# Expert blocks in pairs, 512-wide operations, and the gate/up bias added on DVE

## The reference

```python
gu = jnp.einsum('th,ehf->tef', x, gate_up_proj) + gate_up_proj_bias
gate, up = gu[..., ::2], gu[..., 1::2]
gate = jnp.minimum(gate, LIMIT); up = jnp.clip(up, -LIMIT, LIMIT)
glu = gate * jax.nn.sigmoid(gate * ALPHA)
act = (up + 1.0) * glu
down = jnp.einsum('tei,eih->teh', act, down_proj) + down_proj_bias
out = jnp.einsum('te,teh->th', w, down)
```

## Time and profile before

| | us |
|---|---|
| median of 3 runs (lowest, highest) | 518.12 (512.25, 523.25) |
| the profiled execution: time | 514.28 |
| its span, first to last instruction | 512.5 |
| busy in the span: PE, DVE, POOL, ACT | 389.9, 372.8, 303.0, 221.1 |

### The profile page before, as it was taken

How to read it: one execution, slowest core, us unless ns; L and a number is a source line. 1 busy time by engine, 2 the same in 40 slices (tenths; PEclk the granted TensorE clock), 3 DMA queues, 4 the chain that set the end, 5 groups by cost and what they waited for, 6 DMA issues and landing times.

```text
span 512.5 us, 7809 instructions
## 1 busy us (share of the span) xinstructions
PE 389.9 (76%) x2269; PEld 331.8 (65%) x2269; DVE 372.8 (73%) x861; ACT 221.1 (43%) x480; POOL 303.0 (59%) x260
## 2 busy tenths in 40 slices
PE   0769757224599999999999999981788597888840
PEld 0668657223388889888888988861354386777730
DVE  7897786699387778888788777754997346657640
ACT  3463551000144544445454444531455266778441
POOL 6996890066656677777666667533445242554562
PEclk9866888555599999999999999995689668778665
DMA  6465751000322222322322323306920000111112
GB/s 215 159 203 152 239 149 42 0 0 1 92 74 91 82 88 87 99 91 91 91 87 84 94 72 95 83 25 223 347 87 1 0 1 1 42 41 66 60 41 82
DMA packets 32248, 45.82 MB, mean 89 GB/s; under 512 B 5998, under 2 KB 24818, under 8 KB 32210
## 3 DMA queue, kind: packets, MB, share of 16 engines
q0 software_dynamic: 7968, 21.90, 13.7%
q1 hardware_dynamic: 20018, 19.24, 12.0%
q10 hardware_dynamic: 4224, 4.19, 2.5%
HBM read 28.49 MB, written 17.69 MB: 90 GB/s over the span
## 4 chain that ended last, share of the span: by engine, by line
PE 58%; DVE 21%; ACT 6%; POOL 6%; issue 5%; DMA 3%; SPq 1%; DVEq 0%; POOLq 0%; ACTq 0%
PE bank L885 30%; DVE X L1359 6%; PE bank L882 5%; PE bank L876 3%; PE bank L901 3%; PE bank L846 3%; DVE gu_lo L1114 2%; DVE flow L1205 2%; DVE pair L1201 2%; POOL x_lo L512 2%; POOL pair L515 2%; DVE flow L1110 2%; PE bank L1016 2%; ACT quantT L786 1%; PE bank L825 1%
## 5 line engine op out<-in xcount | busy, mean ns | idle before, releaser
L564 POOL DMA_INDIRECT y_rows<-outs,slot_dst x71 | 71.6, 1009 | 51.2 <-issue 29.9
L544 POOL DMA_INDIRECT rows<-u_rows,slot_src x71 | 71.2, 1003 | 24.8 <-issue 19.2
L692 ACT ACTIVATE tanh<-gate 128x256 f32<-128x256 f32 x71 | 29.6, 417 | 99.8 <-DVE gate L1253 99.8
L885 PE MATMUL bank<-gu_hi,rowT_lo 128*128 x142 | 57.1, 402 | 0.0
L885 PE MATMUL bank<-gu_hi,rowT_hi 128*128 x142 | 56.7, 400 | 0.0
L885 PE MATMUL bank<-gu_lo,rowT_hi 128*128 x142 | 56.4, 397 | 0.0
L1253 DVE TENSOR_SCALAR gate<-bank 128x256 f32<-128x256 f32 x71 | 30.1, 424 | 24.4 <-PE bank L885 24.2
L677 ACT ACTIVATE rowT_hi<-bank 128x256 fp32r<-128x256 f32 x71 | 26.8, 378 | 40.0 <-PE bank L876 40.0
L1359 DVE SCALAR_TENSOR_TENSOR X<-picks,tok_w,X 128x256 f32<-128x256 f32 x64 | 38.9, 673 | 5.8 <-DMA picks<-y_rows 5.5
L1271 DVE TENSOR_TENSOR actT_lo<-bank,actT_hi 128x256 fp32r<-128x256 f32 x71 | 30.1, 424 | 15.3 <-ACT actT_hi L697 14.7
L885 PE MATMUL bank<-dn_lo,actT_hi 128*128 x142 | 40.2, 283 | 0.0
(11 more groups left out here) (268 smaller groups left out, 1196.8 us busy)
## 6 DMA issues: line engine op xcount, KB each, us to landing
picks<-y_rows SPq DMA_DIRECT2D x16, 512.0 KB, 7.2
X<-in_x SPq DMA_DIRECT2D x8, 512.0 KB, 5.7
raw_gu<-in_L_ffn_gate_up_proj SPq DMA_DIRECT2D x8, 512.0 KB, 4.2
u_rows<-flow ACTq DMA_DIRECT2D x8, 512.0 KB, 2.9
out<-X POOLq DMA_DIRECT2D x8, 512.0 KB, 3.4
raw_dn<-in_L_ffn_down_proj SPq DMA_DIRECT2D x8, 256.0 KB, 5.2
rows<-u_rows,slot_src POOLq DMA_INDIRECT x71, 2.8
y_rows<-outs,slot_dst POOLq DMA_INDIRECT x71, 2.5
```

The source lines that it names most:

```text
L544: pool.indirect_dma_start(out=rows[:, s, :], out_offset=None, in_=u_rows, in_offset=bass.IndirectOffsetOnAxis(ap=slot_src[:, n:n + 1], axi ...
L564: pool.indirect_dma_start(out=y_rows, out_offset=bass.IndirectOffsetOnAxis(ap=slot_dst[:, m:m + 1], axis=0), in_=outs[:, m % UNROLL, :], i ...
L692: a.activation(tanh[:, s % 2], gate[:, s % 2], ACT.Tanh, scale=ALPHA).then_inc(tanh_ready, 1)
L885: mm = pe.matmul(acc, left[:, part, :], right[:, ds(expert), part, :].rearrange("p e f -> p (e f)"), start=False, stop=(part == parts - 1 ...
```

## The change

Blocks are taken in pairs: 34 pairs and then 3 single blocks, 37 steps in all (`steps`). The rows' transposes of both blocks go into one bank (4), those of act into one bank (5), each 512 columns, so that ACT and DVE take both blocks in one operation. Gate/up products of the two blocks use two of the four banks 0 to 3, and the down products of the two share bank 6 or 7. The tiles gate, up, tanh, glu, act and actT have one buffer of 512 columns instead of two of 256. The gate/up product has no bias product any more: `gu_bias` now holds the bias in all partitions, put there by one broadcast DMA of SP (128 x 4096 x 4 bytes), and DVE adds it in `biased`, once per block 512 wide, out of PSUM into `gu_sum`, with the block's expert read into a register. The clips read `gu_sum`; the "+ 1" of up moves from the bias into the product with gate. The bias's first DMA, its clearing, splitting and four placing DMAs are gone.

In iteration g, PE does gate/up of the first block of g, the transposes of rows(g+1), down(g−2), gate/up of the second block of g, the transposes of act(g−1). ACT does the rounding of act(g−2), tanh(g−1), the rounding of rows(g+1), outs(g−2). DVE does the sum of the second block of g−1, the remainder of act(g−2), clips and product of g−1, the remainder of rows(g+1), act(g−1), the sum of the first block of g. POOL's loop keeps its order over blocks; its waits count steps. Lines taken away inside rewritten functions are left out below; they are in the listing above.

```diff
@@ -94,6 +94,12 @@
     UNROLL = 8
     NB = (2 * B * S - E) // P + E
     T = B * S
+    PAIR = 2
+    PAIRED = (NB - 2) // 2 * 2
+    steps = [[n, n + 1] for n in range(0, PAIRED, 2)] + [[n] for n in range(PAIRED, NB)]
+    STEPS = len(steps)
+    step_of = {n: g for g, blocks in enumerate(steps) for n in blocks}
+    step_first = lambda g: steps[g][0] if 0 <= g < STEPS else (NB if g >= STEPS else 0)
     GT = 8
     YR = 4
...
-        bank = [ctx.enter_context(nc.psum_tensor(f"bank{i}", [P, 512], F32)) for i in range(8)]
+        gu_banks = ctx.enter_context(nc.psum_tensor("gu_banks", [P, 4, 512], F32))
+        bank = [gu_banks[:, i] for i in range(4)] + [
+            ctx.enter_context(nc.psum_tensor(f"bank{i}", [P, 512], F32)) for i in range(4, 8)]
...
             dn_lo = sb("dn_lo", [P, E, KI, H], F32R)
-            gu_bias = sb("gu_bias", [P, 2, E, I], F32R)
+            gu_bias = sb("gu_bias", [P, E, GU])
             dn_bias = sb("dn_bias", [P, E, H], F32R)
             ones2 = sb("ones2", [P, P], F32R)
...
                 rows = sb("rows", [P, UNROLL, H])
-                rowT_hi = sb("rowT_hi", [P, 2, KH, P], F32R)
-                rowT_lo = sb("rowT_lo", [P, 2, KH, P], F32R)
-                gate = sb("gate", [P, 2, I])
-                up = sb("up", [P, 2, I])
-                tanh = sb("tanh", [P, 2, I])
-                glu = sb("glu", [P, 2, I])
-                act = sb("act", [P, 2, I])
-                actT_hi = sb("actT_hi", [P, 2, KI, P], F32R)
-                actT_lo = sb("actT_lo", [P, 2, KI, P], F32R)
+                rowT_hi = sb("rowT_hi", [P, 2, PAIR * H], F32R)
+                rowT_lo = sb("rowT_lo", [P, 2, PAIR * H], F32R)
+                gu_sum = sb("gu_sum", [P, 2, PAIR * I])
+                gate = sb("gate", [P, PAIR * I])
+                up = sb("up", [P, PAIR * I])
+                tanh = sb("tanh", [P, PAIR * I])
+                glu = sb("glu", [P, PAIR * I])
+                act = sb("act", [P, PAIR * I])
+                actT_hi = sb("actT_hi", [P, PAIR * I], F32R)
+                actT_lo = sb("actT_lo", [P, PAIR * I], F32R)
                 outs = sb("outs", [P, UNROLL, H])
...
-        W_DMAS, BIAS_DMAS, PLACE_DMAS = 2, 2, 6
+        W_DMAS, BIAS_DMAS, PLACE_DMAS = 2, 1, 2
...
@@ -439,16 +447,13 @@
             straight(B, 2, load)
-            sp.wait_ge(bias_step, 5)
-            sp.wait_ge(bias_cleared, 2)
+            sp.wait_ge(bias_step, 2)
+            sp.wait_ge(bias_cleared, 1)
             for half in range(2):
-                for two in range(2):
-                    part = E * GU // P // 2
-                    sp.dma_start(gu_bias[half:half + 1, two].bitcast(F32).rearrange("r e i -> r (e i)"),
-                                 flat_gb[:, half, two * part:(two + 1) * part].bitcast(F32)
-                                 ).then_inc(bias_placed, 16)
                 sp.dma_start(dn_bias[half:half + 1].bitcast(F32).rearrange("r e i -> r (e i)"),
                              flat_db[:, half, :].bitcast(F32)).then_inc(bias_placed, 16)
+            sp.dma_start(gu_bias[:].rearrange("p e f -> p (e f)"),
+                         gate_up_b.rearrange("e f -> (e f)").partition_broadcast(P)).then_inc(gu_bias_loaded, 16)
             sp.wait_ge(rowT_lo_ready, 1)
@@ -540,7 +545,8 @@
             for n in range(NB + AHEAD):
                 if n < NB:
                     s = n % UNROLL
-                    wait_count(pool, rowT_psum, n - UNROLL + 1)
+                    if n >= UNROLL:
+                        pool.wait_ge(rowT_psum, step_of[n - UNROLL] + 1)
                     pool.indirect_dma_start(
                         out=rows[:, s, :], out_offset=None, in_=u_rows,
...
                 if m >= 0:
-                    pool.wait_ge(outs_ready, m + 1)
+                    pool.wait_ge(outs_ready, step_of[m] + 1)
...
@@ -670,47 +676,40 @@
             a.wait_ge(slots_ready, 2)
...
+            def rows_rounded(g):
+                cols = len(steps[g]) * H
+                a.wait_ge(rowT_psum, g + 1)
+                a.activation(rowT_hi[:, g % 2, 0:cols], bank[4][:, 0:cols], ACT.Copy).then_inc(rowT_hi_ready, 1)
+            def activate(g):
+                cols = len(steps[g]) * I
+                a.wait_ge(gate_ready, g + 1)
+                a.activation(tanh[:, 0:cols], gate[:, 0:cols], ACT.Tanh, scale=ALPHA).then_inc(tanh_ready, 1)
+            def transposed_act(g):
+                cols = len(steps[g]) * I
+                a.wait_ge(actT_psum, g + 1)
+                a.activation(actT_hi[:, 0:cols], bank[5][:, 0:cols], ACT.Copy).then_inc(actT_hi_ready, 1)
+            def finish_down(g):
+                blocks = steps[g]
+                a.wait_ge(down_psum, g + 1)
+                for n in blocks:
+                    wait_count(a, outs_stored[n % UNROLL], 16 * (n // UNROLL))
+                first = blocks[0] % UNROLL
+                a.activation(outs[:, first:first + len(blocks), :].rearrange("p b h -> p (b h)"),
+                             bank[6 + g % 2][:, 0:len(blocks) * H], ACT.Copy).then_inc(outs_ready, 1)
+            rows_rounded(0)
+            for g in range(STEPS + 2):
+                if 0 <= g - 2 < STEPS:
+                    transposed_act(g - 2)
+                if 0 <= g - 1 < STEPS:
+                    activate(g - 1)
+                if g + 1 < STEPS:
+                    rows_rounded(g + 1)
+                if 0 <= g - 2 < STEPS:
+                    finish_down(g - 2)
             a.wait_ge(w1_loaded, 48)
...
@@ -869,70 +868,75 @@
                 mm.then_inc(turned, 1)
...
+            def rows_transposed(g):
+                for i, n in enumerate(steps[g]):
+                    pe.wait_ge(rows_loaded[n % UNROLL], 16 * (n // UNROLL + 1))
+                wait_count(pe, rowT_lo_ready, g)
+                for i, n in enumerate(steps[g]):
+                    for half in range(KH):
+                        mm = pe.transpose(bank[4][:, (i * KH + half) * P:(i * KH + half + 1) * P],
+                                          rows[:, n % UNROLL, half * P:(half + 1) * P], ident[:])
                 mm.then_inc(rowT_psum, 1)
...
+            def split_product(acc, hi, lo, w_hi, w_lo, expert, parts, begun):
                 for part in range(parts):
+                    cols = slice(part * P, (part + 1) * P)
                     for left, right in ((hi, w_hi), (lo, w_hi), (hi, w_lo)):
...
+                        mm = pe.matmul(acc, left[:, cols],
                                        right[:, ds(expert), part, :].rearrange("p e f -> p (e f)"),
...
+                                       start=(not begun and part == 0 and left is hi and right is w_hi),
+                                       stop=(part == parts - 1 and right is w_lo))
                 return mm
...
+            experts = {}
+            def gate_up(g, i):
+                d, own = g % 2, slice(i * H, (i + 1) * H)
+                n = steps[g][i]
+                if i == 0:
+                    wait_count(pe, sum_ready, step_first(g - 1))
+                    pe.wait_ge(rowT_lo_ready, g + 1)
+                    for m in steps[g]:
+                        experts[m] = pe.value_load(block_expert[0:1, m:m + 1], min_val=0, max_val=E - 1)
+                mm = split_product(gu_banks[:, 2 * d + i], rowT_hi[:, d, own], rowT_lo[:, d, own], gu_hi, gu_lo,
+                                   experts[n], KH, False)
+                mm.then_inc(gu_psum, 1)
+            def act_transposed(g):
+                pe.wait_ge(act_ready, g + 1)
+                wait_count(pe, actT_lo_ready, g)
+                for i in range(len(steps[g])):
+                    for half in range(KI):
+                        cols = slice((i * KI + half) * P, (i * KI + half + 1) * P)
+                        mm = pe.transpose(bank[5][:, cols], act[:, cols], ident[:])
                 mm.then_inc(actT_psum, 1)
...
+            def down(g):
+                pe.wait_ge(actT_lo_ready, g + 1)
+                wait_count(pe, outs_ready, g - 1)
+                for i, n in enumerate(steps[g]):
+                    own, expert = slice(i * I, (i + 1) * I), experts.pop(n)
+                    acc = bank[6 + g % 2][:, i * H:(i + 1) * H]
+                    pe.matmul(acc, ones2[:], dn_bias[:, ds(expert), :].rearrange("r e h -> r (e h)"), start=True, stop=False)
+                    mm = split_product(acc, actT_hi[:, own], actT_lo[:, own], dn_hi, dn_lo, expert, KI, True)
+                mm.then_inc(down_psum, 1)
             pe.wait_ge(experts_ready, 1)
             pe.wait_ge(slots_ready, 2)
             pe.wait_ge(bias_placed, 16 * PLACE_DMAS)
...
+            rows_transposed(0)
+            for g in range(STEPS + 2):
+                if g < STEPS:
+                    gate_up(g, 0)
+                if g + 1 < STEPS:
+                    rows_transposed(g + 1)
+                if 0 <= g - 2 < STEPS:
+                    down(g - 2)
+                if g < STEPS and len(steps[g]) == 2:
+                    gate_up(g, 1)
```

(62 more changed lines are left out.)

122 lines of the change are left out of this document (4 added, 118 removed).

## The result

The changed kernel takes **610.86 us** (median of 4 runs, 608.13 to 612.30); the kernel before took 520.64 beside it (4 runs, 512.25 to 523.25). The ratio is **1.185, interval 1.171 to 1.199**: slower, as forecast, but 32 us beyond the 579 and outside the range. The profiled execution of after took 612.3, its span 610.6.

A forecast was written before the change was run, and what follows sets the result against it. PE bounds the kernel at 2.89 us a block; after the change a ring through POOL's queue would. The stage adds 63.5 us, the start -0.5: 514.3 becomes 577, or 579 on a mean base; range 565 to 606.

The forecast's parts named there:

- chance of 0.68: Chance given to the forecast itself: the ring at 7.4 to 8.3 us a lap, 564 to 592 us.
- Ring, clean lap: POOL's queue: next pair's gather waits behind a scatter needing outs; 7.88 us a lap instead of 5.79, 30 laps.
- in a third or fewer of the laps: Rival of cold PE: clock drops behind the wait in only some laps, 580 to 600 us; chance 0.15.
- one 3.25 us hole: Evidence against cold PE: clock still 1.00 at 64 to 66 us, inside an idle stretch longer than the ring's 2.5 us.
- price per cold lap: Half clock doubles the ring's transposes and products, 0.43 + 1.52: +1.95 us a lap, +59 over 30; full case 638, chance 0.08.
- Fill: First pairs of the expert stage, before late rows set the laps; outs(0) was to end at 151.0 us.
- called register loads covered: Register loads, the sums and the moved wait for sums hide in each lap's idle time: PE 2.5 us, DVE 3.
- Start of the stage: Before the expert stage, bias memset and one SP issue go: 0.5 us earlier at best, taken as -0.5.
- End: From the end of outs(30) at 387.4 us through last pairs and singles to scatter 70: 22.9 us, so 410.3.
- DVE, ACT: Per pair DVE needs 4.9 us with sums at 0.68 each, ACT's four 512-wide copies 2.4; both hidden under the ring.
- The term for clips beside the gather: 512-wide clips on SBUF may lengthen the ring's gather: up to +0.25 us a lap, 7 in all, for the range only.
- PE-bound, faster: Rival: gather arrives in time before the rows' transposes, pairs take 5.32 us, 505 us on the mean base; chance 0.06.

The follow-up runs named there:

- e1: Changed kernel with scatter n-9 instead of n-8 issued behind gather n (AHEAD 9 instead of 8): 552.71 us, ratio 0.997 to the kernel before.
- e9: Changed kernel with gathers 7 blocks ahead instead of 8 (AHEAD 7): 727.63 us, ratio 1.305 to the kernel before.
- e4: Kernel before, single blocks, with gathers 4 blocks ahead instead of 8: 742.10 us, ratio 1.340 to the kernel before.
- e6: Changed kernel, unchanged, run again beside the kernel before on a later chip: 608.56 us, ratio 1.105.
- e3: Changed kernel plus eight unread 512-wide products on PE before its wait for rows of pairs 4 to 33: 595.53 us, ratio 1.077 to the kernel before.
- e11: Changed kernel plus four unread 512-wide products per pair on PE before its wait for rows: 595.72 us, ratio 1.066 to the kernel before.
- e12: Changed kernel, unchanged, run once more on a third later chip: 611.48 us, ratio 1.086 to the kernel before.
- e7: Changed kernel with scatter n-9 behind gather n and PE's expert register loads moved ahead of its waits: 551.25 us against 550.60 for the kernel before.
- e5: Kernel before, unchanged, profiled again on a later chip: 552.79 us.

## Why the prediction was wrong, and where it was right

Direction and mechanism held; the time did not, and the chance of 0.68 lay on the wrong case. The forecast for the profiled execution's span was 512.5 + 63.0 = 575.5; measured are 610.6, so +35.1 is to be found.

- **Ring, clean lap.** 7.88 forecast, 7.85 to 7.95 in 13 laps, every link within 0.1 (above). 30 waits of PE before the rows, as said. e1, e9 and e4 show the cause: one number in POOL's queue order makes and unmakes it.
- **The failed step: no term for the clock in the sum, "in a third or fewer of the laps" at a chance of 0.15.** The ring was forecast with every lap at full clock; 14 of 29 laps are cold. What their stretch from turned rows to ACT's outs takes beyond 2.33 us adds up to 15.1 of the +19.9 us on the 228.5 (e6 has 14 such laps and 15.0). My evidence against, one 3.25 us hole inside which the clock still was 1.00, was the wrong reading: it told of the clock in the hole, not of the clock that the work behind it got. What the row did show, 0.50 from 68 to 70 behind that hole, was the warning. The price per cold lap was too high: 1.95 forecast, 0.60 to 1.79 in after (mean 1.08), since in most of them the low clock covers only a part of the chain (mean granted clock 0.50 to 0.70 over the first 3.5 us); in e9 it is 1.2 to 1.8 (mean 1.64). Half the laps at about half the price made 15 us, where a third of them at the full price would make 19.5. So this is the largest term that was left out, but not the only one: 20 of the 35 us lie in the terms below. The Trainium skill, "TensorE: Matmul & The Clock Gate", section "HAM oscillation — how this bites in real kernels", tells of a kernel with DMA waits of some 3 to 5 us in which every burst behind one started cold. The trace agrees for the holes of 4.1 to 6.5 us in e9, in all laps. For the holes here, shorter than the page's, it happened in 14 of 29 laps.
- **The rest of the laps' +19.9**, 4.8 us: 2.4 for one late scatter, 1.0 for the late rows of the two laps named above (the same two laps have them in e3 and e11: 8.60 and 8.59, 8.33 and 8.55), and about 0.05 in each lap. The late scatter, in after's ACT and POOL timelines:

```profile
380.58 0.60 ACT L700 ACTIVATE outs<-bank 128x512 f32<-128x512 f32 x1 [2.36 <-PE bank L886]
```

```profile
384.38 1.14 POOL L570 DMA_INDIRECT y_rows<-outs,slot_dst  x1 [6.73 <-issue]
```

  From the end of outs to the scatter are 3.20 us, not 0.80. It is scatter 52, the 114th indirect DMA of POOL, and e3, e6, e11 and e12 have 3.20 or 3.21 at the same one. So has the kernel before (outs ends at 295.46, the scatter starts at 298.67): the delay is not the change's, but only the ring makes it cost time. Its cause is open.
- **Fill: +5.3.** From rows of pair 0 to rows of pair 4 I had 21.4 us; it took 26.7. In after's timeline the low part of the first rows ends at 141.72 + 0.69 = 142.41, and the first gate/up product starts 1.76 later:

```profile
141.72 0.69 DVE L1233 TENSOR_TENSOR rowT_lo<-bank,rowT_hi 128x512 fp32r<-128x512 f32 x1 [5.85 <-ACT rowT_hi L682]
...
144.17 0.79 PE L886 MATMUL gu_banks<-gu_hi,rowT_hi 128*128 x1 [3.27 <-issue]
```

  PE loads two expert numbers there with nothing queued to cover them. I had called register loads covered, which holds in the ring and not in the fill. e7 takes 2.7 of the 5.3 away by loading earlier (15.42 us for the first three laps against 18.08 in after and in e1). The rest is small waits in the first two pairs (0.95 at 150.74, 0.62 for DVE's act and 0.89 at 156.39).
- **Start of the stage: +5.7**, not the change's. The first gather starts at 135.5 in after, 130.3 in before, and anywhere from 129.8 to 137.0 in the other profiles, with the old start code (e4 137.0, e5 136.8) as with the new. The changed start itself, priced at −0.5, can't be told apart from that. The 2 MB broadcast landed in 10.0 us, not on the path, as said.
- **End: +2.9 and +1.3.** From rows of pair 33 to the last scatter 28.65, where my chain had 25.8; behind the last scatter nothing of the change runs.
- **DVE, ACT.** The sum takes 0.688 (0.68 taken; the bounds 0.42 and 0.85 held), the 512-wide clips 0.43 and 0.47, ACT's copies 0.60. None sets a lap of the ring.
- **The term for clips beside the gather** came to nothing in the ring: the gathers in it took 0.97 to 1.05. But the effect is there. In after 14 scatters and one gather began 0.04 to 0.33 us behind the start of a 512-wide DVE operation on SBUF. They took 1.11 to 1.53 us instead of 1.00, and each ended 0.86 to 0.89 behind the end of that operation:

```profile
183.43 0.69 DVE L1256 SCALAR_TENSOR_TENSOR glu<-up,gate 128x512 f32<-128x512 f32 x1
183.48 1.53 POOL L570 DMA_INDIRECT y_rows<-outs,slot_dst  x1 [0.30 <-issue]
```

  All but one of these scatters (384.38 above) were the second of a pair, outside the ring, and so cost it nothing. The Trainium skill's rule ("SBUF — State Buffer", section "🔬 SBUF: two separate sides") has such a DMA wait for DVE; by these lengths the trace agrees, though it does not name the mode of the DVE operations.
- **Two roundings of the prediction.** Pairs at 5.32 give 504 on the mean base, not 505, and 0.4 us less in each of 30 laps gives 567, not 565. Neither bears on the miss.

+5.7 + 5.3 + 19.9 + 2.9 + 1.3 = 35.1.

"PE-bound, faster" had its price right, since out of the ring PE's shortest lap was 5.34; but on these chips it gave no time that can be told from none, and in the first result's setting it was not run.

## What to carry to other kernels

When a change doubles the grain of a pipeline, walk every in-order queue in the new order and ask for each entry what the one in front of it now waits for; the fix may be one number in that order. A wait that recurs in front of TensorE had two prices here, the wait and the half-speed work behind it: put the second into the sum and not into a rival, and test it by giving the engine useless work. And when a stretch has no cover (a fill), count the register loads.

## What the runs showed of the hardware that I had not expected

- PE's clock was at its lower level (1.2 GHz) for part or all of the chain of transposes and products behind the hole in 14 laps of after. The holes in front of these were 2.05 to 2.77 us, and 4.69 once. In 15 laps it was at the upper level (2.4 GHz), with holes of 1.47 to 2.12 us. With four useless products more per lap the mean clock stood at 0.99, and half of each hole was still there (1.0 to 1.5 us in most laps).
- An indirect DMA of POOL that began just behind a 512-wide DVE operation on SBUF ended 0.86 to 0.89 us behind that operation, up to 1.53 us after its own start. Where the two began within 0.03 to 0.05 us of each other, often the DVE operation took longer instead: `glu` 0.75 to 0.77 and the scatter 1.00 to 1.02.
- The same program of before took 520.6 us in the first result and 551 to 559 on three chips later, while the changed kernel took 609 to 611 in three places. So a ratio from one chip is not the ratio of another.
- Scatter 52, the 114th indirect DMA on POOL, started 2.4 us late in before, after, e3, e6, e11 and e12; in e4, where the 114th is scatter 54, that one did.
